# One block for the first attention and the first expert layer: expert units inside the attention's tail, expert 0's weights split during the attention, another order of chunks

## What is computed

```python
x = x + jnp.tanh(g_xattn[0]) * _L0_xattn_ref(_layernorm(x, axis=-1), ctx_1024, ctx_1024, ...)
x = x + jnp.tanh(g_ffn[0]) * _L0_ffn_ref(_layernorm(x, axis=-1), ...)
x = x + jnp.tanh(g_xattn[1]) * _L1_xattn_ref(_layernorm(x, axis=-1), ctx_1024, ctx_1024, ...)
x = x + jnp.tanh(g_ffn[1]) * _L1_ffn_ref(_layernorm(x, axis=-1), ...)
```

```python
h1 = jnp.einsum('ebcm,emh->ebch', dispatch, w1)
h3 = jnp.einsum('ebcm,emh->ebch', dispatch, w3)
expert_out = jnp.einsum('ebch,ehm->ebcm', jax.nn.silu(h1) * h3, w2)
```

## Time and profile before

| | us |
|---|---|
| time, median of 3 runs | 1816.24 |
| lowest and highest | 1811.12, 1818.09 |
| span of the profiled execution | 1875.6 |
| PE busy in it | 1608.9 (86%) |
| DVE busy | 1249.7 (67%) |
| ACT busy | 984.2 (52%) |
| POOL busy | 763.9 (41%) |

### The profile page before, as it was taken

One profiled execution on the slowest core, in us unless ns is written; L12 is line 12 of the kernel. 1 busy time (PEld: TensorE's weight loads), 2 busy tenths in 40 slices (PEclk: granted clock), 3 DMA queues, 4 the chain that ended last, 5 costly groups with the idle time before them and its releaser, 6 DMA issues. The chain is left out here.

```text
span 1875.6 us, 44921 instructions
## 1 busy us (share of the span) xinstructions
PE 1608.9 (86%) x16664; PEld 1233.1 (66%) x16664; DVE 1249.7 (67%) x3643; ACT 984.2 (52%) x1728; POOL 763.9 (41%) x932
## 2 busy tenths in 40 slices
PE   4599999757999999999996688898876898888884
PEld 3355666436888888888884455665643787777752
DVE  4678887735556565565556889889883566556656
ACT  4477877534444454444432455666543575555531
POOL 2155657875401010010034534423642445566643
PEclk8799999877999999999998899999988998999997
DMA  9853433214655535545232433323335366778733
GB/s 290 217 117 69 72 66 66 55 44 125 186 177 192 183 111 198 177 133 183 65 100 77 103 83 84 83 53 63 81 88 193 133 226 205 240 242 265 230 113 95
DMA packets 297706, 257.02 MB, mean 137 GB/s; under 512 B 198047, under 2 KB 270155, under 8 KB 296216
## 3 DMA queue, kind: packets, MB, share of 16 engines
q1 hardware_dynamic: 271256, 168.84, 32.9%
q0 software_dynamic: 26240, 85.32, 13.4%
HBM read 102.98 MB, written 107.74 MB: 112 GB/s over the span
## 5 line engine op out<-in xcount | busy, mean ns | idle before, releaser
L1649 PE MATMUL ps<-m_xT,m_w_halves 128*128 128x256 f16 x3360 | 414.0, 273 | 1.1 <-issue 1.0
L1649 PEld LDWEIGHTS ps<-m_xT,m_w_halves 128*128 128x128 f16 x3360 | 329.5, 98 | 40.7 <-issue 1.9
L1161 ACT ACTIVATE a_probs<-ps 128x1024 f32<-128x1024 f32 (+1 forms) x256 | 234.6, 917 | 167.1 <-PE ps L994 160.1
L1668 PE MATMUL ps<-m_w_halves,m_hiddenT 128*128 128x256 f16 x1680 | 229.2, 273 | 5.6 <-DVE m_hiddenT L1764 5.6
L1277 POOL TENSOR_TENSOR a_probs<-a_probs,a_half_above 128x512 f32<-128x512 f32 x128 | 162.2, 1270 | 151.4 <-ACT a_probs L1161 150.9
L1725 ACT ACTIVATE m_hiddenT<-m_hidden 128x256 f16<-128x256 f32 x280 | 116.6, 416 | 197.2 <-DVE m_hidden L1761 194.7
L1764 DVE TENSOR_TENSOR m_hiddenT<-m_hidden,m_hiddenT 128x256 f16<-128x256 f32 x280 | 119.0, 425 | 134.9 <-ACT m_hiddenT L1725 131.1
L994 PE MATMUL ps<-a_Q,a_K 32*128 32x256 f16 (+1 forms) x2048 | 147.5, 263 | 68.1 <-DVE a_neg_max L1359 32.5
L1616 POOL DMA_DIRECT2D expert_out<-m_y x40 | 28.9, 722 | 434.1 <-DVE m_y L1744 431.5
L1362 DVE TENSOR_REDUCE a_qT<-ps 128x4 f16<-128x1024 f32 x128 | 156.5, 1222 | 47.9 <-PE ps L1005 46.9
L994 PEld LDWEIGHTS ps<-a_Q,a_K 32*128 32x128 f16 x2048 | 82.6, 94 | 152.4 <-issue 62.6
(11 more groups left out here) (320 smaller groups left out, 3030.9 us busy)
## 6 DMA issues: line engine op xcount, KB each, us to landing
routed<-m_zeros POOLq DMA_DIRECT2D x32, 768.0 KB
r_space<-routed SPq DMA_DIRECT2D x48, 512.0 KB
routed_out<-m_y SPq DMA_DIRECT2D x48, 512.0 KB
r_w_load<-in_L_w SPq DMA_DIRECT2D x24, 896.0 KB
dispatched<-r_xT SPq DMA_DIRECT2D x10, 1024.0 KB, 6.5
expert_out<-m_y POOLq DMA_DIRECT2D x40, 256.0 KB
a_ctx_in<-in_ctx SPq DMA_DIRECT2D x32, 256.0 KB
m_experts_load<-in_L_experts SPq DMA_DIRECT2D x18, 384.0 KB, 3.5
```

The costliest lines, as they stand in the source:

```text
L1161: A(pr[:, g % 2, 2 * jp:2 * jp + 2, :], SC[:, :, 0:SPAN], ACT.Exp, scale=1.0 / math.sqrt(DH)).then_inc(asem["ex"], 1)
L1649: last = mm(psum[:, v % HB, m * CH:(m + 1) * CH], wh[:, u, ws_, m, d_ * F0 + f_ * P:d_ * F0 + (f_ + 1) * P], xT[:, q % XB, xs_ * KT + d_, ...
L1668: last = mm(psum[:, 4 + 2 * (q % 2) + t, 0:D], hT[:, hs_, f_, t * P:(t + 1) * P], wh[:, u, ws_, 2, f_ * D:(f_ + 1) * D], start=f_ == 0 and ...
```

## The change

`moe0` becomes a class `FirstExperts` whose methods `sync`, `gpsimd`, `tensor`, `scalar` and `vector` are called from inside `attention(0)`'s block. There is no barrier between the two stages any more. Since both now live in the same block, the attention's buffers are given up at once (`stack.close()` right after they were set up) and the expert layer's buffers are laid over them; waits in `split_upper`, `load`, `hidden` and `down` keep them apart. The weights of the attention's projections wq, wk, wv move to the attention's own buffers for this.

- Expert 0's six weight pieces are split in the slots (13,3) to (14,5), on DVE one slot later. The splits of expert 1 move from the units 8 to 13 to the units 0 to 5, those of expert 2 from 52 to 67 to 58 to 68.
- Units 0 to 7 stand at the ends of the slots of i = 16, units 8 to 15 in those of i = 17, on PE, ACT and DVE. The others follow.
- In the first five chunks (`APART`) the two halves of `down` write two PSUM banks without doubling. The second half runs three units later than the first, and the result is taken in two copies.
- The chunks of experts 0 and 1 alternate. Block 3 is needed from chunk 6 on instead of chunk 5.
- The routing of block 2 is placed two slots later. Its scatters run in the slots (17,7) to (18,2) and after. That of sequences 14 and 15 and of block 3 stands in the units 22 to 34, and block 3's scatters stand in one run on POOL.
- SP loads expert 1's weights ahead of the first chunks, behind the attention's own transfers.

```diff
-ROUTE_PLACE = {10: (0, 4), 14: (1, 4), 17: (2, 5)}
+ROUTE_PLACE = {10: (0, 4, 2), 14: (1, 4, 2), 17: (2, 4, 4)}
-ROUTE_SCATTER = {11: (0, 0, 4), 12: (0, 4, 4), 13: (0, 8, 4), 14: (0, 12, 4), 15: (1, 0, 4), 16: (1, 4, 8), 17: (1, 12, 4)}
+ROUTE_SCATTER = {11: (0, 0, 4), 12: (0, 4, 4), 13: (0, 8, 4), 14: (0, 12, 4), 15: (1, 0, 4), 16: (1, 4, 8), 17: (1, 12, 8)}
+SPLIT_FIRST = {(13, 3): 0, (13, 5): 1, (13, 7): 2, (14, 1): 3, (14, 3): 4, (14, 5): 5}
...
+                        if not causal_band and i >= B:
+                            first.tensor(pe, 8 * (i - B) + s)
+                if not causal_band:
+                    for unit in range(16, first.LAST + 2):
+                        first.tensor(pe, unit)
...
+                        if not causal_band and (i, s) in SPLIT_FIRST:
+                            first.split_upper(act, 0, SPLIT_FIRST[i, s])
...
+                    if not L and (i, s) in ((B + 1, 7), (B + 2, 0), (B + 2, 1), (B + 2, 2)):
+                        for j in range(2):
+                            route_scatter(pool, 2, 2 * (8 * (i - B) + s - 15) + j)
...
-        ORDER = [(0, 0), (0, 1), (1, 0), (1, 1), (0, 2), (0, 3), (0, 4), (1, 2), (1, 3), (1, 4)] + \
...
-        BLOCK_AT = {0: 0, 1: 1, 4: 2, 5: 3}
-        WEIGHTS_AT = {FT + 1 + i: (1, i) for i in range(6)}
-        WEIGHTS_AT.update({7 * FT + 3 * (i + 1): (2, i) for i in range(6)})
+            ORDER = [(0, 0), (1, 0), (0, 1), (1, 1), (0, 2), (1, 2), (0, 3), (0, 4), (1, 3), (1, 4)] + \
...
+            BLOCK_AT = {0: 0, 2: 1, 4: 2, 6: 3}
+            WEIGHTS_AT = {i: (1, i) for i in range(6)}
+            WEIGHTS_AT.update({8 * FT + 2 + 2 * i: (2, i) for i in range(6)})
...
-                for p in range(STEPS + 1):
-                    for v in range(p * FT, (p + 1) * FT):
-                        j = v + 4
-                        if j < 4 * RT:
-                            pool.wait_ge(h_done, v + 1)
-                            route_scatter(pool, 2 + j // (2 * RT), j % (2 * RT))
+                for q in range(STEPS):
+                    if q >= 2:
+                        store(q)
+                    if q == 3:
+                        for j in range(2 * RT):
+                            route_scatter(pool, 3, j)
...
+                if unit == 25:
+                    pe.wait_ge(xT_out, 14)
+                    route_transposes(pe, 0, 14, 4)
+                    pe.wait_ge(asem["xnew"], B * PER["xnew"])
+                    route_transposes(pe, 0, 15, 7)
+                if unit == 28:
+                    route_logits(pe, 3, 4)
+                if unit == 32:
+                    route_positions(pe, 3, 7)
+                if unit < LAST:
+                    hidden(unit)
+                if 0 <= unit - 5 < V0:
+                    down(unit - 5, 1)
+                if unit >= 2:
+                    down(unit - 2, 0)
```

## The result

| | before | after |
|---|---|---|
| time, median (lowest to highest) | 1815.29 (1811.12 to 1818.09), 4 runs | 1843.45 (1840.46 to 1845.36), 4 runs |
| ratio, 95% interval | 1 | 1.0152 [1.0133, 1.0171] |
| unit 42 starts, in the profile | 526.43 | 551.91 |
| from unit 42 to the last unit's start | 468.6 | 468.1 |

The forecast was 1816, in a range up to 1830; the kernel takes 1843. The page's first part shows nothing of it: the engines' busy times are those of before but for 15 us more on ACT and 9 less on PE.

What follows compares the result with a forecast made beforehand. TensorE, busy 86%, was taken as the limit, with idle time at the seam between attention and experts. The steps put unit 42 at 526.1 against 526.43, 0.3 us faster: 1816 us, range 1794 to 1830.

Steps and rivals of the forecast that it cites:

- What has no price of its own: Shifted zero stores, expert 2's later splits and its weights queued on SP: taken as covered; an uncovered load would cost 8 us.
- Units 16 to 27: PE work to 471.8, but block 2's scatters, transposes and landing on POOL and SP hold unit 28 until 475.8.
- Units 33 to 41: Block 3's rows take 30.7 us from unit 33, PE needs 17.7; unit 42 comes at 521.1 before clock and restart.
- Block 3's stall: Ahead of unit 42, PE stands still 13.0 us for block 3's sixteen scatters and their transposes.
- Attention's end: Six weight splits in sequences 13 and 14 lengthen attention by 3 us, bounds 0 and 6.6; unit 0 at 393.
- Units 0 to 15: Woven into attention's tail: 29.75 us for units 0 to 7 (DVE limits), 20.65 for 8 to 15 (PE limits).
- The clock rival: Low clock persists in units 0 to 7, deciding below 0.81: up to 18 us more, 1833; chance 0.12.
- The restart: At unit 42, PE loses 3 us to low clock after 13 us of rest, bounds 1.5 and 5.
- The scatter rival: Block 3's sixteen scatters on POOL each take 1.92 with overhead, 10.4 us more: 1826; chance 0.08.
- The faster rival: Block 3's rows arrive in time for unit 42; stall and restart, 16 us, go: 15.5 us better, 1800; chance 0.30.
- ACT's table loads: Four added switches on ACT at 1.28 us each, 5.1 in all; with the skill's drain 10.6, near 1821.
- the late input: Unit 0's transposes, behind expert 1's weight loads on SP, land 6 us late and shift everything: 1822; chance 0.05.

Runs made afterwards that it cites:

- e4_loads: The kernel of e1_stores with the loads of the next layer's first two expert weights on SP ahead of chunk 4's transposes; 1826.97 us, ratio 1.0049.
- e3_route: The kernel of e1_stores with block 3's routing and scatters earlier and the second next-layer load ahead of block 3's transposes; 1817.14 us, ratio 1.0023.
- e5_route: The kernel of e3_route with both loads of the next layer's weights on SP ahead of chunk 4's transposes; 1813.17 us, ratio 0.9979.
- the second profile: The kernel before, unchanged, profiled again; measured 1816.54 us, profile span 1814.7.
- e1_stores: The kernel after with chunk 0's store on POOL ahead of sequence 13's lower half and chunk 1's ahead of block 2's last eight scatters; 1846.72 us, ratio 1.0182.

## Why the prediction was wrong, point by point

`e4_loads` is the kernel after with the two queue orders mended.

| step | predicted | after | `e4_loads` |
|---|---|---|---|
| unit 0 starts at | 393 | 398.7 | 394.5 |
| unit 0 to 16 | 50.4 | 54.0 | 53.6 |
| unit 16 to 28 | 32.4 | 44.2 | 32.3 |
| unit 28 to 33 | 14.6 | 16.5 | 16.2 |
| unit 33 to 42 | 30.7 | 38.5 | 32.5 |
| added for clock and restart | 5 | in the steps | in the steps |
| unit 42 starts at | 526.1 | 551.9 | 529.1 |

**The step that failed** is the sentence that begins "What has no price of its own". It named stores of zeros, expert 2's splits and expert 2's weights as what stands behind the moved scatters. Two more things stand there, and neither was walked: the stores of chunks 0 and 1 on POOL, behind block 2's scatters, and the loads of the next layer's weights on SP, behind the transposes of blocks 2 and 3. Each has a consumer with a fixed place in another queue (DVE's L1836 behind unit 21, ACT's L1793 ahead of units 25 and 39). With them mended, 16 to 28 and 33 to 42 come to 32.3 and 32.5, and unit 42 to within 3 us of the sum. That is closer than the working deserves: the steps ran 8 us over in `e4_loads`, and the 5 added for clock and restart took up most of it. The steps "Units 16 to 27" and "Units 33 to 41" priced their own chains nearly right, and missed that another wait on each would end later: 11.8 and 7.8 us. I had asked of each moved issue who waits for its result, but not who stands behind it.

**Block 3's stall**, the decisive step by the prediction, was right in kind and size: forecast 13.0, measured 12.74 in `e4_loads`. Its terms in the kernel after: rows known 5.4 us behind unit 33 (4.4 predicted); sixteen scatters 20.5 (20.3); seen 1.5 later (1.5); transposes 3.3 (2.5); and from there to unit 42 another 7.8, in place of 2. That last one holds the load that ACT waited for; the trace gives no landing for these two transposes (in `e4_loads` block 3's landed 4.2 and 2.9 us after their issue).

**Attention's end** was mis-sized: 3 us, with 6.6 as the upper bound. The last exponential starts at 397.24 instead of 388.34, 8.9 later; unit 0 followed at 398.7, 2.1 past the bound. The five other profiles with the same attention have unit 0 at 391.6 to 396.1, inside it, so the overrun is partly this one profile's (last section). DVE's timeline shows how a lower half (L1816) stands in front of a reduction (L1390) for which, through PE's L1005, the next exponential waits, and takes 1.68 us there instead of the 1.09 of the earlier trace rows:

```profile
359.17 1.68 DVE L1816 TENSOR_TENSOR m_w_halves<-r_w_load,m_w_halves 128x896 f16<-128x896 f32 x1
360.77 1.22 DVE L1390 TENSOR_REDUCE a_qT<-ps 128x4 f16<-128x1024 f32 x1
```

**Units 0 to 15** came to 54.0 for 50.4, all of it in units 0 to 7 (33.4 for 29.75, within the bounds given for the waits there); units 8 to 15 took 20.6 for 20.65. The 3.90 us that PE waited at 427.37 and the slice at half clock behind it are the nearest rows; no run tested them.

**The clock rival** didn't happen: the granted clock from unit 0 to unit 16 is 0.91, over the 0.81 from which it was to decide, though a slice of 4 us is at 0.50, or 1.2 GHz.

```profile
398.71:452.71 54.00, 44.05 (x370) 37.03 (x367) 30.25 (x99) 26.65 (x54) 21.31 (x32) 0.91 0.13 40
```

```profile
428.00:432.00 4.00, 4.00 (x21) 2.88 (x20) 2.62 (x15) 1.33 (x4) 0.00 (x0) 0.50 0.27 72
```

**The restart** was priced at 3; from unit 42 to 43 it is 3.57 us instead of 1.965, so 1.6.

**The scatter rival** didn't happen either. In `e3_route`, where PE hardly paused beside them, the 16 took (count, ns min/median/max, first and last start):

```profile
L379 POOL DMA_INDIRECT dispatched<-r_x_halves,r_scatter_row x16: 967/972/1110, 499.2 to 518.6; - x16
```

The Trainium skill, "SBUF — State Buffer", section "Who interferes with whom", says that a VectorE instruction with two SBUF inputs contends with a GpSimd instruction that reads SBUF; beside the units' subtracts on VectorE these rows show no such lengthening. The longest scatter of that profile, 1.85 us at 422.48, ran beside a weight subtract, as the 1.62 of before did, and there it stays open.

**The faster rival**, block 3 in time, was priced at 16 us of profile, 15.5 of time. `e5_route` shows 13.8. In the kernel as written it did not happen.

**ACT's table loads.** A switch to the exponential and back took two loads of 1.28, each with an ACTIVATE right behind it and the work ahead of it ended at 417.07:

```profile
416.14 0.93 ACT L1779 ACTIVATE m_w_halves<-r_w_load 128x896 f16<-128x896 f32 x1
417.09 1.28 ACT L305 ACT_TABLE_LOAD   x1
418.38 0.26 ACT L305 ACTIVATE r_probs<-r_logits 128x64 f32<-128x64 f32 x1
418.66 1.28 ACT L1797 ACT_TABLE_LOAD   x1
419.95 0.38 ACT L1797 ACTIVATE m_silu<-ps 128x256 f32<-128x256 f32 x1
```

So the sum of loads alone was right here. The drain of 1.38 that the Trainium skill, "ScalarE: Activation LUTs", section "What ACT_TABLE_LOAD costs", adds to each doesn't show in these rows, whose gaps are 0.01 to 0.02 us.

**Profile time and timed time.** The factor 0.968 spread the first profile's extra 60 us evenly. They lay behind the first expert layer, so a microsecond at the seam is a microsecond of time. By the second profile the loss adds up: unit 42 is 25.9 later (551.9 against 526.0), the units from there to the last take 2.4 more (468.1 against 465.7; the prediction had this at nothing), what follows takes 0.3 more (823.23 against 822.95): 28.6, the difference of the spans 1843.2 and 1814.7 but for rounding.

**The chances.** Slower had 0.25. Of what it rested on, the clock, the scatters and the late input did not occur; the upper edge of the sum did in part (5.7 us at unit 0, 3.6 in units 0 to 15). The neighbours in a queue had been priced at zero; the one figure given for them, 8 us for a load that isn't hidden, entered neither the range nor the chances. And none of the signs named for the slow side at units 0 to 15 came (clock 0.91, unit 16 at 452.7), while the kernel was slower.

## What to carry to other kernels

When a block of issues with a late wait is moved, write down for each queue it stands in what comes behind it, and for each of those who waits for it and when: a store behind scatters holds a buffer, a prefetch behind a waiting transfer holds the engine that is to use it, even where both belong to other work. Where two such waits hang on the same event, mending one can show nothing, as `e1_stores` did; mend both before you judge the mechanism. A prefetch whose data is ready belongs ahead of transfers that wait, not behind them.

## What was not expected of the hardware

Two transposes issued at 551.89 and 553.92 in the kernel after, behind those of block 3, took 6.5 and 5.0 us from issue to landing, where the median over all landings of transposes in the profile is 2.8. The DMA engines were busy there, at a share of 1 and more (last but one column). That the one comes of the other is not tested.

```profile
DMA to landing us min/median/max: 5.0/5.8/6.5
```

```profile
552.00:554.00 2.00, 2.00 (x11) 1.42 (x10) 1.19 (x3) 0.94 (x3) 0.00 (x0) 0.50 1.00 379
554.00:556.00 2.00, 2.00 (x15) 1.56 (x13) 0.42 (x1) 0.80 (x2) 0.00 (x0) 0.70 1.37 157
```

And unit 0, ahead of which six of these kernels run the same attention, started at 391.6, 394.5, 395.1, 396.1, 396.1 and 398.7 us in their profiles. In the latest of them, the kernel after, PE had a slice with gaps at 380 and then one fully busy with 27 matmuls at 0.51, where the next slice did 45 at full clock in less busy time; in the earliest, `e1_stores`, the slices from 380 to 396 are all at 1.00. The rows of the kernel after:

```profile
380.00:384.00 4.00, 2.88 (x27) 1.18 (x26) 0.14 (x1) 2.39 (x4) 3.40 (x7) 0.50 0.45 111
384.00:388.00 4.00, 4.00 (x27) 2.16 (x20) 0.00 (x0) 1.97 (x3) 2.33 (x2) 0.51 1.02 407
388.00:392.00 4.00, 3.60 (x45) 2.03 (x42) 1.53 (x5) 2.67 (x5) 2.52 (x2) 1.00 1.11 323
```

A difference of a few microseconds at unit 0 between two single profiles of this program is therefore no evidence on an edit.
